# Group-norm, pooled-gate convolution block: thirteen image slots, half-slot reloads and stores, and one kept slot for each of nine samples

## What is computed

```python
def _gn(v, G=32, eps=1e-5):                    # statistics over a whole sample, per group of 24 channels
    ...
def conv_block(x):                             # 768 -> 16 -> 768 channels
    xc = conv1x1(x, conv1_w, conv1_b)          # R = 16 channels
    g = softmax(top2(mean_pixels(xc) @ H_w.T + H_b))
    for i in range(4):                         # upsample by 2**i, 3x3 convolution, downsample
        up = resize(xc, 2**i); up = conv3x3(up, convl_w, convl_b); Es[i] = resize(up, back)
    out = sum_i Es[i] * reshape(g, (4, 16, 1, 1, 1))[i]
    return conv1x1(out, conv2_w, conv2_b)      # back to 768 channels
x = x + conv_block(_gn(x))
```

## Time and profile before

| what | value |
|---|---|
| median of 3 runs | 1641.06 us (1640.28 to 1644.9) |
| the profiled execution, its own time | 1641.5 us |
| its span, first to last instruction | 1639.8 us |
| bytes moved | 593.46 MB, 362 GB/s over the span |
| read from memory, written to it | 390.60 MB, 201.33 MB |
| PE (matmul) busy | 1222.1 us, 75% |
| DVE busy | 1039.3 us, 63% |
| ACT busy | 657.6 us, 40% |
| POOL busy | 352.7 us, 22% |

### The profile page before, as it was taken

One profiled execution on the slowest core, in us unless ns is written; L12 is line 12 of the kernel. 1 busy time (PEld: TensorE's weight loads), 2 busy tenths in 40 slices (PEclk: granted clock), 3 DMA queues, 4 the chain that ended last, 5 costly groups with the idle time before them and its releaser, 6 DMA issues.

```text
span 1639.8 us, 23721 instructions
## 1 busy us (share of the span) xinstructions
PE 1222.1 (75%) x8700; PEld 845.3 (52%) x8700; DVE 1039.3 (63%) x2763; ACT 657.6 (40%) x1549; POOL 352.7 (22%) x359
## 2 busy tenths in 40 slices
PE   1758879887889595949798968689597877766463
PEld 1636656655656363636565646366364544434231
DVE  7859765667576758555767575776845563453453
ACT  3758883444544453635454445435242100000000
POOL 2063008304010000052404100431004844211000
PEclk9889999989998797969889988799698887768555
DMA  9767774999999999957999999999999699999999
GB/s 359 270 230 273 280 298 157 397 350 406 367 406 397 409 398 409 393 222 289 400 343 392 379 408 378 406 335 410 410 402 403 237 403 411 415 413 415 414 414 381
DMA packets 203047, 593.46 MB, mean 362 GB/s; under 512 B 10290, under 2 KB 10290, under 8 KB 202932
## 3 DMA queue, kind: packets, MB, share of 16 engines
q1 hardware_dynamic: 202932, 591.95, 92.8%
HBM read 390.60 MB, written 201.33 MB: 361 GB/s over the span
## 4 chain that ended last, share of the span: by engine, by line
DMA 45%; PE 28%; DVE 11%; SPq 7%; issue 3%; ACT 2%; POOL 2%; DVEq 0%; ACTq 0%; POOLq 0%
DMA x_sb<-in_x 37%; PE ring_ps L613 11%; DMA out<-x_sb 8%; DVE x_sb L915 7%; PE img_ps L626 5%; SPq L427 5%; PE conv_ps L678 5%; PE ring_ps L707 5%; DVE stats L835 1%; POOL band L563 1%; PE ring_ps L695 1%; POOL taps L564 1%; ACT xT L725 1%; SPq L436 1%; PE ring_ps L638 1%
## 5 line engine op out<-in xcount | busy, mean ns | idle before, releaser
L915 DVE TENSOR_TENSOR x_sb<-x_sb,ring_ps 128x768 f32<-128x768 f32 x512 | 456.8, 949 | 358.1 <-PE ring_ps L707 188.4
L835 DVE BATCH_NORM_STATS2 stats<-x_sb 128x6 f32<-128x192 f32 x1792 | 472.5, 343 | 126.1 <-DMA x_sb<-in_x 68.5
L725 ACT COPY xT<-ring_ps 128x1024 f32<-128x1024 f32 x384 | 365.9, 1016 | 226.1 <-PE ring_ps L613 225.4
L613 PE MATMUL ring_ps<-ident,x_sb 128*128 128x128 f32 x3072 | 390.5, 285 | 72.7 <-DMA x_sb<-in_x 41.2
L707 PE MATMUL ring_ps<-w,es 128*128 128x512 f32 (+1 forms) x1024 | 322.6, 437 | 161.5 <-DVE x_sb L915 145.6
L613 PEld LDWEIGHTS ring_ps<-ident,x_sb 128*128 128x128 f32 x3072 | 354.5, 147 | 130.4 <-issue 88.6
L707 PEld LDWEIGHTS ring_ps<-w,es 128*128 128x128 f32 x1024 | 190.6, 229 | 275.2 <-DVE x_sb L915 152.3
L626 PE MATMUL img_ps<-xT,w 128*32 128x256 f32 x3072 | 219.9, 401 | 65.5 <-DVE w L866 55.0
L577 POOL TENSOR_TENSOR band<-taps,masks 128x640 f32<-128x640 f32 x112 | 169.7, 1541 | 444.0 <-PE conv_ps L678 442.8
L678 PE MATMUL conv_ps<-xc,band 128*128 128x1 f32 (+8 forms) x1120 | 219.9, 345 | 34.3 <-POOL band L577 20.5
L678 PEld LDWEIGHTS conv_ps<-xc,band 128*128 128x128 f32 x1120 | 156.1, 195 | 106.6 <-issue 93.4
(11 more groups left out here) (94 smaller groups left out, 341.8 us busy)
## 6 DMA issues: line engine op xcount, KB each, us to landing
x_sb<-in_x SPq DMA_DIRECT2D x248, 1536.0 KB, 18.5
out<-x_sb SPq DMA_DIRECT2D x128, 1536.0 KB, 12.9
w_rep<-in_L_conv_conv_w SPq DMA_DIRECT2D x8, 48.0 KB, 10.3
bias<-in_L_conv_conv_b SPq DMA_DIRECT2D x8, 0.1 KB, 10.0
wl_raw<-in_L_conv_convl_w SPq DMA_DIRECT2D x8, 9.0 KB, 7.0
bias_l<-in_L_conv_convl_b SPq DMA_DIRECT2D x8, 0.1 KB
gate_w<-in_L_conv_H_w SPq DMA_DIRECT2D x8, 0.2 KB
w_raw<-in_L_conv_conv_w SPq DMA_DIRECT2D x1, 48.0 KB
```

The lines of the kernel that those rows point to most:

```text
L613: last = nc.tensor.transpose(ring_ps[:, buf, q, half * P:(half + 1) * P], slot("L", a, 2 * c + half)[:, q, k * P:(k + 1) * P], ident[:, :])
L725: nc.scalar.copy(xT[:, at % XT], ring_ps[:, TURN["T", a, n] % RING]).then_inc(xT_copied, 1)
L835: ins = nc.vector.bn_stats(stats[:, c, g, :], two_slots(n0, n1, g))
L915: nc.vector.tensor_tensor(x_sb[:, n, q, :], x_sb[:, n, q, :], flat_ps[:, TURN["E", b, t] % RING, 0:D], ALU.add).then_inc(added, 1)
```

## The change

- `SLOTS` 12 to 13. The room comes from smaller buffers: `XT` 4 to 3, `BANDS` 4 to 3, `w1`, `pick`, `masks`, `experts` in tighter layouts.
- `KEPT` has one piece (piece 0) of each of samples 0, 1, 2, 3, 5, 6, 7, 10 and 11 beside the eight of sample 15: 17 kept pieces instead of 8, so 111 pieces are reloaded instead of 120.
- A reload and a store now move half a piece (two of its four tiles). Each half slot has its own `loaded` and `stored` semaphores. The two halves of a reloaded piece may lie in different slots. First loads stay whole.
- The weights' transfers are issued by ScalarE (ACT) before its first other work, no longer by SP.
- The four lists are written anew.
- POOL: expert 0 has 3x3 taps of its own tile (`expert_0`, 144 numbers) and is added last; for the matrices TOP and BOTTOM the band is cleared and one of its eight blocks (80 numbers) is multiplied, in place of one product of 640.
- `spread` contracts over 32 partitions instead of 128 (same 512 columns, same number of matmuls). `fold` writes `w1` once instead of twice.

```diff
-SLOTS = 12
+SLOTS = 13
-XT = 4
+XT = 3
-BANDS = 4
+BANDS = 3
-KEPT = {15: 8}
+KEPT = {0: 1, 1: 1, 2: 1, 3: 1, 5: 1, 6: 1, 7: 1, 10: 1, 11: 1, 15: 8}
 TRANSFERS = """
-L4.0:0 L4.1:1 L4.2:2 W1 L4.3:3 L4.4:4 L4.5:5 L4.6:6 L4.7:7 L8.0:8 L8.1:9 L8.2:10 L8.3:11 L8.4:6 L8.5:7 L8.6:4 L8.7:5
-W2 L12.0:2 L12.1:3 L12.2:0 L12.3:1 L12.4:4 L12.5:5 L12.6:6 L12.7:7 L0.0:10 L0.1:11 L0.2:8 L0.3:9 L0.4:6 L0.5:7 L0.6:4
+L4.0:0 L4.1:1 L4.2:2 L4.3:3 L4.4:4 L4.5:5 L4.6:6 L4.7:7 L8.0:8 L8.1:9 L8.2:10 L8.3:11 L8.4:12 L8.5:6 L8.6:7 L8.7:4
+L12.0:5 L12.1:2 L12.2:3 L12.3:0 L12.4:1 L12.5:4 L12.6:7 L12.7:6 L0.0:12 L0.1:10 L0.2:11 L0.3:8 L0.4:9 L0.5:6 L0.6:7
...
-                sp.dma_start(x_sb[:, n], x_v[s, i // 4, i % 4]).then_inc(loaded[n], 16)
...
+                        sp.wait_ge(stored[half], 16 * stores[half])
+                if kind == "L":
+                    sp.dma_start(x_sb[:, n[0]], x_v[s, i[0] // 4, i[0] % 4]).then_inc(loaded[n], 16)
+                else:
+                    half = slice(2 * i[1], 2 * i[1] + 2)
+                    sp.dma_start(x_sb[:, n[0], 2 * n[1]:2 * n[1] + 2], x_v[s, i[0] // 4, i[0] % 4][:, half]
+                                 ).then_inc(loaded[n], 16)
...
-                sp.wait_ge(added, BI[s] * TILES + (i + 1) * QN)
-                sp.dma_start(out_v[s, i // 4, i % 4], x_sb[:, n]).then_inc(stored[n], 16)
+                sp.wait_ge(added, BI[s] * TILES + i[0] * QN + 2 * i[1] + 2)
+                sp.dma_start(out_v[s, i[0] // 4, i[0] % 4][:, 2 * i[1]:2 * i[1] + 2],
+                             x_sb[:, n[0], 2 * n[1]:2 * n[1] + 2]).then_inc(stored[n], 16)
...
         @block.scalar
         def _(act):
+            for h in range(NH):
+                rows = slice(R * h, R * h + R)
+                act.dma_start(w1_rep[rows, :], conv1_w.rearrange("r c y x -> r (c y x)")).then_inc(weights_in, 16)
+                act.dma_start(bias_1[rows, 0:1], conv1_b.unsqueeze(1)).then_inc(weights_in, 16)
...
+            act.wait_ge(bias_zero, 1)
+            for row in (64, 96):
+                act.dma_start(b2_raw[row:row + 1, :], conv2_b.unsqueeze(0)).then_inc(late_weights_in, 16)
             act.wait_ge(consts_ready, 1)
...
-                for p in range(2):
-                    ins = nc.vector.tensor_tensor(w1[:, at, :, p, p * R:(p + 1) * R], w1T[:, :, :],
-                                                  of_channel[:, :].unsqueeze(2).broadcast_to([P, KB, R]), ALU.mult)
-                ins.then_inc(w1_ready, 1)
+                nc.vector.tensor_tensor(w1[:, at, :, R:2 * R], w1T[:, :, :],
+                                        of_channel[:, :].unsqueeze(2).broadcast_to([P, KB, R]), ALU.mult
+                                        ).then_inc(w1_ready, 1)
...
+                    blocks = slice(0, 1) if m == TOP else slice(NH - 1, NH) if m == BOTTOM else slice(0, NH)
+                    if m in (TOP, BOTTOM):
+                        link(nc.gpsimd.memset(band[:, n % BANDS], 0.0))
```

More of the change, by code:

```diff
@@ L418, in _ @@
         def _(sp):
-            def load(kind, s, i):
-                n, _, before = loads[kind, s, i]
-                if before is not None:
-                    was, s0, i0 = before
-                    if was == "L" and i0 >= KEPT.get(s0, 0):
-                        sp.wait_ge(transposed, AI[s0] * STEPS + (CHUNKS - i0 // 2) * KB)
-                    else:
-                        sp.wait_ge(stored[n], 16 * stores[n])
-                sp.dma_start(x_sb[:, n], x_v[s, i // 4, i % 4]).then_inc(loaded[n], 16)
@@ L473, in _ @@
+            for half in stored:
+                if stores[half]:
+                    sp.wait_ge(stored[half], 16 * stores[half])
         @block.gpsimd
```

403 lines of the change are left out of this document (219 added, 184 removed).

## The result

| | before | with the change |
|---|---|---|
| median | 1640.99 us (4 runs, 1640.28 to 1644.9) | 1556.07 us (4 runs, 1552.47 to 1560.48) |
| profiled execution, its span | 1641.5, 1639.8 us | 1560.48, 1558.8 us |
| bytes moved | 593.46 MB | 579.34 MB |
| span less bytes at 414 GB/s | 206 us | 159 us |

The ratio is 0.9479, with a 95% interval of 0.945 to 0.9509: 85 us faster. The last row of the table is a measure used all through what follows: 593.46 MB need 1433.5 us at 414 GB/s, so 206 us of the span are *unfilled*. Of the 81 us between the two spans, 34 are bytes and 47 are unfilled time that went. (The profiled execution is the slowest of the four with the change; the median is 4 us shorter.)

The account below looks back on a forecast made before the run. Transfers were taken to bound the kernel outside the opening and holes, and the chain PE, statistics, fold to bound the opening. Terms -34.2 - 10.5 + 1.5 - 4 - 3 - 2 + 5 = -47.2 took 1641.5 to 1594 us, range 1576 to 1620.

Parts of the forecast that it names:

- nine reloads less: Mixed stretches with a full queue: 14.16 MB fewer at 414 GB/s save 34.2 us.
- halves (transfers +5, holes -2): 230 more transfers cost 5 us; first stores leaving a half slot earlier in the holes save 2 us.
- weights (-10.5 and +1.5): Opening: sample 12's long period shortens by 10.5 us; ACT issuing weights first delays its first square root, +1.5 us.
- POOL, single `w1`, smaller `spread`: POOL's shorter work saves 3 us in the holes; one `w1` product counted within `Z`'s -4; smaller `spread` 0.
- rings of three: Three `xT` buffers cost 0, hidden by PE's other steps (28 us if not); the three-band ring was counted within POOL's -3.
- thirteenth slot: Brings nothing beyond the kept pieces, since each occupies a slot from its load to its store.
- `Z`: Opening: `Z` ahead of the last projection step, with one `w1` product gone, saves 4 us over four periods.
- the holes as long as before: Sign expected in the profile after: holes in the transfer queue keep their length; under rival A they are longer.
- Rival A: Saved bytes vanish in the waits: half the nine slots' time only lengthens a hole, 17 us lost, 1611 us; 15%.
- Rival B: Each transfer has a fixed price of 0.11 us: +20 us against the forecast, 1614 us; 9%.
- Rival D: Last part: half reloads wait for stores in a ring of four slots, 84 us over some 30 rounds, 1678 us; 5%.
- Rival C: Opening stays as long, through ACT's late start or the three buffers: 13 us more, 1607 us; 6%.

Follow-up runs that it names:

- 13 slots: Changed code with the kernel before's four lists, rings of three and its kept pieces, given 13 slots instead of 12: 1611.5 us, ratio 0.9807.

## Why the prediction was wrong

The direction and the number for the bytes were right. The size was short by 38 us. Two terms make up most of it, the halves and the lists.

| part | predicted | measured |
|---|---|---|
| nine reloads less | -34.2 | -36 under the new lists, +2.5 under the old |
| halves (transfers +5, holes -2) | +3 | -16 |
| weights (-10.5 and +1.5) | -9 | -3 under the old lists, 0 under the new |
| POOL, single `w1`, smaller `spread` | -3 | -7 |
| rings of three | 0 | 0 |
| thirteenth slot | 0 | -5 |
| the new lists at equal bytes, `Z` among them | -4 | -20 |
| sum | -47 | -87, by the medians -85 |

The measured parts are steps of one chain from the kernel before to the change, so they must add up; in another order single parts would differ, as the bytes show.

*The lists* are the step that failed first. The prediction read three places of them, gave `Z` its -4, and took the rest as neutral: "the holes as long as before". It had found the hole of 697 to 779 us and said what ends it ("when a chain of gates, convolution and adds is done"). That was right, 32 us before and after. It did not ask when the last output before it was written. That question has an answer in the trace of before, 39 us of DVE without an add ahead of the gates, and the lists of the change say what becomes of them. With equal bytes the lists gave 20 us (1611.5 to 1592.05). The stages put 12 us of gain into the middle hole and 16 into the last one, which the prediction left standing at 237 GB/s and which is gone; part is given back elsewhere. Reading DVE's adds around each set of gates would have pointed at both.

*The bytes* came out right, but the reason given, that the queue is full where the reloads stand, does not carry the number. The old lists have a busy share of 1.02 there too, and the same nine reloads dropped from them brought nothing. That the new lists could use the time was not argued, so this hit was in part luck.

*The halves* had the wrong sign. The price of a transfer was bounded from rows in which packets of four bytes stand, and taken at +5; in the last stretch it doesn't show at all, 414 GB/s against 414. What was missed is the gain. It was counted only in the holes, as two adds or 1.8 us in each (by that working three holes are -5 and not -2), and 12 of the 16 us came from the mixed work between the holes. There, too, stores wait for their adds and reloads for the store in their slot. The gain needs both ends: alone, half stores cost 9 us and half reloads gave 3.

*The slot*: the prediction's argument was that a kept piece occupies what the slot adds. By itself the slot is worth 5 us. The same argument points to the real question, whether nine kept pieces starve an order made for twelve slots, and under the old lists they did, with slots given out by the greedy rule.

*The opening* came out at nearly the right sum from wrong parts. The fifth fold came 13.7 us earlier (236.2 to 222.5 us), where -10.5, +1.5 and -4 make 13; some 2 us of that are only its place in DVE's list, where the pooled gates now stand behind it. The sum is met by luck. But ACT came to its statistics at 36.5 us and not at 30, which put the first fold 7.4 us back (46.7 to 54.1) and not 1.5. In exchange the ordinary period fell by 2.3 us, from 43.3 to 41.0, where `Z` and one `w1` product had been given 1 us. Not all of it is the lists: the granted clock of the period was 0.92 before and 0.96 with the change. The same period with the old lists at 0.96 (13 slots) and with the new lists at 0.92 (weights on SyncE):

```profile
145.22:187.63 42.41, 37.33 (x392) 27.85 (x392) 33.17 (x133) 35.77 (x92) 0.00 (x0) 0.96 0.81 299
145.18:186.78 41.60, 37.68 (x392) 28.84 (x392) 33.16 (x132) 34.94 (x88) 0.00 (x0) 0.92 0.80 299
```

So at one clock the lists are worth some 1.5 us of the 2.3, and the rest goes with the clock. The period of sample 12, at 44.1, is near the 45.3 of the sum, yet most of what it gave was lost at the start.

*Rival A*, the saved bytes vanish in the waits, is false for the change and true for the same code with the old lists, where all 34 us went and not the half that the rival priced. It had 15%; its mechanism hung on a part that the prediction took as neutral. *Rival B* fell with the rate of the last stretch. The Trainium skill's rule in *DMA: Bandwidth & Descriptors*, Bandwidth, of at least 1 MiB for three quarters of the peak fell with it: the halves are 0.75 MiB and move at 410 to 414 GB/s, one behind the other in a full queue. *Rival D*, reloads in a ring of four slots run dry, would have shown as a share under 1 in the stretch of 1394 to 1541 us, which has 1.03. There it costs at most 147 x (1 - 410/414) = 1.4 us, and the same stretch of the kernel with the weights on SyncE has 413. After the last hole as a whole the new lists leave 9 or 10 us unfilled and the old ones 4 or 5, so a ring that runs dry at the very end could cost some 5 us; no run settles that. *Rival C*, the opening as long as before, fell with the fifth fold.

The range was built from the bounds of the terms that were listed. It had no room for a term that wasn't: lists read in three places only. Even with every term at its better end the sum gives 1583, and not 1580. Of the smaller sums, POOL's pair of 144 numbers took 1.13 us and not 0.84, while the clears brought the 1.0 us that was taken for them.

## What to carry to other kernels

Where a program has points at which nothing can be written until a result is known, look at what the list does in the time before that point, and in the time from it to the first output that uses the result: outputs held back for these times keep slots and transfers going, and a plan that finishes early stands still. Saved bytes are worth their time only if the order of the work can use it, so price them together with the order; here the same nine pieces were worth +2.5 or -36 us. Halving a unit helped where both the transfer that frees the room and the one that fills it were halved; with only one of them it gave 3 us or cost 9.

## What the runs showed of the hardware

*A queue that takes only so much.* The changed kernel's first thirteen loads wait for no semaphore. The summary of that line in 0 to 60 us (duration ns min, median, max, then first and last start; below, time from issue to landing) shows that issuing them takes long all the same:

```profile
L471 SPq DMA_DIRECT2D x_sb<-in_x x13: 434/4042/9617, 0.8 to 42.0; - x13
...
DMA to landing us min/median/max: 7.0/21.0/25.6
```

The shortest issue is 0.43 us, the median 4.04 us, which is about the time in which one load passes (1.573 MB at 390 GB/s is 4.0 us). The likely reading is that SyncE stands in front of a full queue until a load has passed; then 21 us to landing by 4 us a load is some five whole loads under way at once. By this reading a time from issue to landing is mostly the queue's length, and an "idle" issuing engine after a row of big transfers is not idle.

*No price for a half transfer, with one exception.* With 606 transfers (624 in the kernel before with both halves) in place of 376, the rate of the last stretch stayed at 410 to 414 GB/s. The exception is half stores between whole reloads, 504 transfers, at 402 GB/s and a share of 1.02, which stays unexplained. The Trainium skill says of trn2 in *DMA: Bandwidth & Descriptors*, Anatomy of one DMA, a section on transfers issued by GpSimd, that the bubble of a semaphore write is tiny; the last stretch with both halves agrees, at 414 GB/s and a share of 1.03.
